# Attention and mixture of experts in one kernel: two buffers for the turned rows of the projections, and the first routing spread over the second attention

## The chip, the cores and the metric

The kernel runs on one NeuronCore of a Trainium2 chip. Its engines are TensorE (PE in the rows; PEld is its weight load), VectorE (DVE), ScalarE (ACT), GpSimd (POOL) and SyncE (SP), which here only issues transfers. Each engine works through its own list of instructions in order, and waits for semaphores that the others raise. The metric is the time of one execution on the device in microseconds, smaller is better. The time before is 1181.86 us, the median of three runs (1181.4 to 1183.72).

## The reference

Two sequences of 2048 rows of 256 values pass through one attention head (width 128, rotary positions), and then twice through a mixture of eight experts with the two best chosen per row:

```python
# x: [2, 2048, 256]
x = x + layernorm(attn(layernorm(x), wq, wk, wv, wo))
x = x + layernorm(ffn(layernorm(x), norm_w, router_w, w1, w3, w2))

# attn: q, k, v = x @ wq.T, x @ wk.T, x @ wv.T; rotary on q, k from the second row on
w = softmax(q @ k.T / sqrt(128)); out = (w @ v) @ wo.T

# ffn, LOOPS = 2 times over z, E = 8 experts, F = 512
z_norm = z * rsqrt(mean(z * z) + 1e-6) * norm_w
scores = softmax(z_norm @ router_w); vals, idx = top_k(scores, 2)
vals = vals / (sum(vals) + 1e-9)
z = z + sum_e vals_e * ((silu(z_norm @ w1[e]) * (z_norm @ w3[e])) @ w2[e])
```

## The kernel before

**Stages.** The first block of the program handles sequence 0 and then sequence 1: projections, then attention. A second block runs the four expert passes (two loops by two sequences, 39 tiles of 128 rows each), which take two thirds of the time and which the change leaves as they are but for names. A sequence is 16 tiles of 128 rows; the projections take them in 8 pairs. Every number that goes through a product is split into two halves of 16 bits, a high one and the rest (`_hi` and `_lo` functions), and each product is made as three matmuls.

**A pair of the projections.** ScalarE normalises two tiles into `xn` (`x_norm`, L760), TensorE transposes them into the bank `psum_t[0]` (`turn_x`, L1225), ScalarE writes the high half of the one buffer `xT` (`x_hi`, L766), VectorE the rest (`x_lo`, L1029). Then come 12 matmuls (`qkv`, L1235) into two banks, one for each tile. From each bank ScalarE takes v (`v_hi`, L772), VectorE the rest of v (L1037) and the products for the rotation (L1045), and GpSimd adds those up (`rotate`, L660, L661). TensorE transposes the turned q and k (`turn_qk`, L1245), ScalarE and VectorE store them as halves (`qk_hi`, L778; `qk_lo`, L1054). On TensorE pair n is written as `qkv(n)`, then `turn_x(n + 1)`, then `turn_qk(n - 1)`: the next pair is transposed only after the matmuls that read `xT`.

In sequence 1 the same pairs also carry work for the experts. ScalarE scales the high halves of two groups of expert weights for each pair (`split_pair`, `split_hi`, L787); the rest of the even group is made on GpSimd (`split`, L671, L675), that of the odd group on VectorE (`split_lo`, L1021). TensorE transposes x for the router (`first_turn`, L540), ScalarE copies it (`copy_zT`, L580), TensorE makes the logits (`logits`, L565). GpSimd computes two roots (L330, L334).

**A step of the attention.** Step t makes the scores of tile t (L1258), transposes the probabilities of tile t - 1 in four groups (`turn_p`, L1253), projects tile t - 2 (L1283) and multiplies the probabilities of t - 1 with v (L1291). VectorE takes the maxima (L1065, L1082), the low halves of the transposed probabilities (`p_lo`, L1060) and the statistics of the result (L1089, L1094). ScalarE makes the exponentials (L832) and high halves (L783, L815), and normalises the result (L818) once GpSimd's chain (`normalise`, L684 to L694) gives the root. GpSimd adds it to x (L696). Steps 3 to 15 are a hardware loop on each engine.

**The first routing.** In the second attention VectorE runs `first_routing` and the five functions of `place` as one block of about 70 small instructions, between its work for steps 0 and 1. ScalarE stands still until it is done:

```python
                if last:
                    exps(act, 0)
                    act.wait_ge(s_eid, 1)
```

Then VectorE marks, for each of 32 halves of tiles, which lane a token goes to (`mark_lanes`, L494): six in step 2 and two in each later step. TensorE sums the marks at the end (`tokens_of_rows`, L502) and VectorE turns the sums into row numbers (`row_indices`, L512 to L518). Meanwhile ScalarE scales each row tile for the experts (`first_row_of`, L802), GpSimd splits it into the one buffer `first_split` (`first_rows`, L706, L708) and SyncE stores it, one tile in each step from step 1 to 16.

## Time and profile before

| | before |
|---|---|
| time, median of 3 runs | 1181.86 us |
| the profiled execution's own time | 1178.43 us |
| its span on the core | 1176.6 us |
| TensorE busy | 1047.3 us, 89% |
| VectorE busy | 738.3 us, 63% |
| ScalarE busy | 579.2 us, 49% |
| GpSimd busy | 530.8 us, 45% |

The shares are means over stages that have different limits. All starts are counted from the start of the span. The projections of sequence 0 run from 14.7 to 51.2 us, the first attention to 190.9, the projections of sequence 1 to 246.6, the second attention to 398.3; the experts take the rest. A number in the clock column below 1.00 means that for a part of that stretch TensorE ran at the lower of its two clocks.

### The profile page before, as it was taken

What the parts mean: (1) busy time and instruction counts of PE and PEld (TensorE: products, weight loads), DVE (VectorE), ACT (ScalarE), POOL (GpSimd) and SP (SyncE); (2) the same over time, 40 slices, a digit from 0 to 9 for tenths busy, and PEclk for the clock granted to TensorE, in tenths of its full rate; (3) what the DMA queues carried; (4) which work ended last, traced back from release to release, by engine and by line L of the source; (5) the groups of instructions that cost most, each with busy time, mean ns of one, the idle gap of its engine ahead of it and who ended that gap; (6) DMA issues with size and microseconds to landing.
All of it is one profiled execution on the core that took longest, in us unless ns stands there. A gap on an engine that the chain in (4) does not pass through costs nothing.

```text
span 1176.6 us, 25481 instructions
## 1 busy us (share of the span) xinstructions
PE 1047.3 (89%) x7762; PEld 705.7 (60%) x7763; DVE 738.3 (63%) x1671; ACT 579.2 (49%) x1124; POOL 530.8 (45%) x699
## 2 busy tenths in 40 slices
PE   5699897758999499999999999999999999999930
PEld 3476675536777366666666666666766666666620
DVE  6799998859999344476345466444467536544436
ACT  4466565627888334453345464344454333333312
POOL 3312234834777553344444444444354444554315
PEclk9999999969999799999999999999999999999975
DMA  9900000000000133354365354355445446433344
GB/s 319 324 1 0 0 0 1 1 0 15 18 15 16 50 74 77 81 143 110 90 162 140 79 141 114 90 136 142 110 125 128 91 121 162 123 92 90 81 141 163
DMA packets 146309, 110.78 MB, mean 94 GB/s; under 512 B 92592, under 2 KB 132144, under 8 KB 146224
## 3 DMA queue, kind: packets, MB, share of 16 engines
q1 hardware_dynamic: 131248, 68.72, 23.2%
q0 software_dynamic: 14976, 40.91, 11.8%
q8 instruction: 55, 0.90, 0.3%
q14 instruction: 30, 0.25, 0.1%
HBM read 56.11 MB, written 33.03 MB: 76 GB/s over the span
## 4 chain that ended last, share of the span: by engine, by line
PE 61%; DVE 2%; DMA 1%; issue 1%; ACT 0%; POOL 0%; ACTq 0%; SPq 0%; DVEq 0%; POOLq 0%
PE psum_s L1869 35%; PE psum_o L1888 17%; PE psum_s L1877 6%; PE psum_t L565 2%; PE psum_t L1831 1%; DVE arena L1661 1%; DMA arena<-expert_rows 0%; DVE f_stats L1687 0%; DMA arena<-arena 0%; DMA arena<-sorted_rows,token_of_row 0%; DVE arena L1667 0%; DMA expert_rows<-arena,result_row_of_row 0%; PE psum_t L502 0%; DVE f_tmp L341 0%; ACT arena L1646 0%
## 5 line engine op out<-in xcount | busy, mean ns | idle before, releaser
L1869 PE MATMUL psum_s<-w_all,arena 128*128 x1872 | 432.8, 381 | 12.1 <-DMA arena<-arena 11.2
L1536 POOL DMA_INDIRECT expert_rows<-arena,result_row_of_row x156 | 157.0, 1007 | 356.7 <-ACT arena L1621 354.9
L1869 PEld LDWEIGHTS psum_s<-w_all,arena 128*128 128x128 f16 x1872 | 174.2, 98 | 212.9 <-issue 22.4
L1791 DVE SCALAR_TENSOR_TENSOR arena<-psum_s,gate_scale,arena 128x512 f32<-128x512 f32 x156 | 117.1, 750 | 205.3 <-PE psum_s L1869 201.2
L1888 PE MATMUL psum_o<-w_all,arena 128*128 x1872 | 229.8, 273 | 1.5 <-DVE arena L1784 1.5
L1888 PEld LDWEIGHTS psum_o<-w_all,arena 128*128 128x128 f16 x1872 | 181.7, 98 | 47.9 <-issue 3.6
L1784 DVE TENSOR_TENSOR arena<-psum_s,arena 128x512 f16<-128x512 f32 x156 | 107.5, 689 | 148.2 <-ACT arena L1610 147.4
L1621 ACT ACTIVATE arena<-psum_o 128x256 f32<-128x256 f32 x156 | 59.8, 383 | 251.3 <-PE psum_o L1888 251.3
L1527 POOL DMA_INDIRECT arena<-sorted_rows,token_of_row x156 | 153.4, 983 | 52.1 <-issue 45.7
L1615 ACT ACTIVATE arena<-psum_s,silu_scale 128x512 f32<-128x512 f32 x156 | 107.2, 687 | 123.1 <-PE psum_s L1869 123.0
L1610 ACT ACTIVATE arena<-psum_s 128x512 f16<-128x512 f32 x156 | 93.1, 597 | 20.0 <-PE psum_s L1877 14.0
L1291 PE MATMUL psum_o<-arena 128*128 128x128 f16 x1536 | 96.6, 220 | 4.1 <-DVE arena L1060 2.0
L832 ACT ACTIVATE arena<-psum_s,arena,alpha 128x1024 f32<-128x1024 f32 x64 | 76.5, 1199 | 38.9 <-DVE arena L1082 38.7
L1291 PEld LDWEIGHTS psum_o<-arena 128*128 128x128 f16 x1536 | 89.4, 98 | 9.6 <-DVE arena L1060 8.8
L1877 PE MATMUL psum_s<-ident,arena 128*128 128x128 f32 x624 | 94.1, 273 | 0.8 <-DVE arena L1791 0.8
L1258 PE MATMUL psum_s<-arena 128*128 128x512 f16 x384 | 91.7, 390 | 1.4 <-DVE arena L1054 1.4
L783 ACT ACTIVATE arena<-psum_t 128x512 f16<-128x512 f32 x128 | 69.9, 595 | 46.3 <-PE psum_t L1253 32.0
L1060 DVE SCALAR_TENSOR_TENSOR arena<-psum_t,arena 128x512 f16<-128x512 f32 x128 | 81.9, 680 | 5.2 <-ACT arena L783 4.8
L1065 DVE TENSOR_REDUCE arena<-psum_s 128x1 f32<-128x1024 f32 x64 | 77.5, 1214 | 8.6 <-PE psum_s L1258 8.6
L1253 PE MATMUL psum_t<-ident,arena 128*128 128x128 f32 x512 | 69.7, 279 | 9.7 <-DVE arena L1060 6.8
L1877 PEld LDWEIGHTS psum_s<-ident,arena 128*128 128x128 f32 x624 | 73.5, 143 | 3.2 <-DVE arena L1791 1.6
L1253 PEld LDWEIGHTS psum_t<-ident,arena 128*128 128x128 f32 x512 | 57.5, 143 | 19.5 <-DVE arena L1060 6.8
(235 smaller groups left out, 1119.6 us busy)
## 6 DMA issues: line engine op xcount, KB each, us to landing
w_all<-in_L_ffn_w SPq DMA_DIRECT2D x24, 512.0 KB, 10.1
arena<-expert_rows SPq DMA_DIRECT2D x48, 256.0 KB, 3.4
sorted_rows<-w_all SPq DMA_DIRECT2D x24, 256.0 KB, 2.6
arena<-expert_rows SPq DMA_DIRECT2D x8, 512.0 KB, 6.0
out<-x_sb SPq DMA_DIRECT2D x8, 512.0 KB, 6.8
...
```

Source lines behind the costliest of these rows:

```text
L1253: last = nc.tensor.transpose(psum_t[g % 2][:, k * P : (k + 1) * P], probs[:, kc * P : (kc + 1) * P], ident[:, :])
L1258: last = nc.tensor.matmul(psum_s[:, kb * 512 : (kb + 1) * 512], qkT[:, lq, 0, bass.ds(i * P, P)], qkT[:, lk, 1, kb * 512 : (kb + 1) * 512] ...
L1291: last = nc.tensor.matmul(psum_o[:, 0:P], v_tiles[:, kc, lv, :], pT[:, lp, at], start=(kc == 0 and k == 0), stop=(kc == NT - 1 and k == 2))
L1527: nc.gpsimd.indirect_dma_start(x_pair[:, u, :, :].rearrange("p l d -> p (l d)"), None, x_split[h], bass.IndirectOffsetOnAxis(ap=sources[:, ...
L1536: nc.gpsimd.indirect_dma_start(expert_rows[h][:, :], bass.IndirectOffsetOnAxis(ap=targets[:, h, t : t + 1], axis=0), y_row[:, u, :], None) ...
L1610: nc.scalar.activation(hT[:, 0, :, :].rearrange("p c t -> p (c t)"), psum_h, ACT.Copy).then_inc(s_h_hi, 1)
L1615: nc.scalar.activation(silu_a, psum_a, ACT.Silu, scale=silu_scale[:, 0:1]).then_inc(s_silu, 1)
L1784: nc.vector.tensor_tensor(hT[:, 1, :, :].rearrange("p c t -> p (c t)"), psum_h, hT[:, 0, :, :].rearrange("p c t -> p (c t)"), ALU.subtract ...
L1791: nc.vector.scalar_tensor_tensor(h_row, psum_b, gate_scale[:, 0:1], silu_a, ALU.mult, ALU.mult).then_inc(s_h, 1)
L1869: last = nc.tensor.matmul(bank, e_xT[:, u, lx * DC + c, :], w_split[:, bass.ds(e * EW + at, FF)], start=(q == 0), stop=(q == 3 * DC - 1))
L1877: last = nc.tensor.transpose(psum_h[:, c * P : (c + 1) * P], h_row[:, c * P : (c + 1) * P], ident[:, :])
L1888: last = nc.tensor.matmul(psum_e, hT[:, lh, c, :], w_split[:, bass.ds(e * EW + at, D)], start=(q == 0), stop=(q == 3 * FC - 1))
```

## The change

- **Two buffers for turned rows.** `xT` becomes a pair of buffers, the second lying where `pT` is in the attention. TensorE is given `turn_x(n + 1)` ahead of `qkv(n)`; ScalarE does `x_hi(n + 1)` ahead of `v_hi(n)` and `x_norm(n + 2)` behind it; VectorE does `x_lo(n + 1)` first.
- **High halves of odd groups.** In the projections of sequence 1 VectorE makes them itself (`split_hi`, seven of them); ScalarE keeps the even ones. They get a semaphore of their own.
- **Scratch for the first routing.** Its tiles no longer share words with probabilities, so they can live through steps. The block is cut up: `first_factors` goes to the end of the projections, the constants and `shifted_logits` behind step 0, the softmax and the first pick behind step 1, the second pick and the gates behind step 2, `tiles_before`, `expert_starts` and `expert_rows_of_tiles` behind step 3, `rows_of_tokens`, `experts_of_tiles` and `mark_tiles` behind step 4. Lanes are marked four in a step, in steps 5 to 12. The sums of tokens and the row numbers come in step 14. Steps 3, 4, 13, 14 and 15 are written out on VectorE and no longer in the loop. ScalarE no longer waits for `s_eid`.
- **Rows for the experts.** `first_split` becomes two buffers; the rows start in step 0, two each in steps 1 and 2, and end in step 13.

```diff
         xn = take(2 * D).rearrange("p (u d) -> p u d", u=2)
-        first_row, first_split = xn[:, 0, :], xn[:, 1, :].bitcast(F16)
-        xT = take(2 * 2 * D // 2).bitcast(F16).rearrange("p (l u c t) -> p l u c t", l=2, u=2, c=DC)
+        first_row = xn[:, 0, :]
+        xT_words = (take(2 * 2 * D // 2), pT[:, 0, :].bitcast(F32)[:, 0 : 2 * D])
+        xT = [w.bitcast(F16).rearrange("p (l u c t) -> p l u c t", l=2, u=2, c=DC) for w in xT_words]
+        first_split = (xn[:, 1, :].bitcast(F16), xT_words[0][:, 0:D].bitcast(F16))
...
+        FIRST_ROWS = [(0,), (1, 2), (3, 4)] + [(i + 2,) if i < NT - 2 else () for i in range(3, NT + 4)]
...
-            v_hi(0, 0)
-            x_hi(1)
-            act.wait_ge(s_shift_x, 2)
-            for i in range(1, PAIRS):
-                if i < PAIRS - 1:
-                    x_norm(i + 1, i + 1)
-                v_hi(i, i)
+            for i in range(PAIRS):
                 if i < PAIRS - 1:
                     x_hi(i + 1)
-                qk_hi(i - 1, i - 1)
+                v_hi(i, i)
+                if i == 0:
+                    act.wait_ge(s_shift_x, 2)
+                if i < PAIRS - 2:
+                    x_norm(i + 2, i + 2)
+                if i:
+                    qk_hi(i - 1, i - 1)
...
+            def split_hi(n):
+
+                if n > 1:
+                    dve.wait_ge(s_w_lo_v, (n - 1) // 2)
+                nc.vector.tensor_scalar(w_split[:, n * 2 * GROUP : n * 2 * GROUP + GROUP], w_raw[:, n * GROUP : (n + 1) * GROUP],
+                                        scale_g[:, :, :].rearrange("p e g -> p (e g)")[:, n : n + 1], None,
+                                        ALU.mult).then_inc(s_w_hi_v, 1)
...
             step(NT, True, False, False, False, False)
-            split_lo(FIRST_SPLITS + 1)
-            first_routing()
-            for place_step in place:
-                place_step(dve, link, 0)
+            routing_constants()
+            shifted_logits(dve, link, 0)
+            split_lo(odd(0))
             step(NT + 1, True, True, False, False, False)
-            split_lo(FIRST_SPLITS + 3)
+            softmax(dve, link, 0)
+            pick_best(dve, link, 0, 0)
+            split_lo(odd(1))
+            step(NT + 2, True, True, True, False, False)
+            pick_best(dve, link, 0, 1)
+            gate_values(dve, link, 0)
+            split_lo(odd(2))
+            step(NT + 3, True, True, True, True, False, 0, read_counts)
+            tiles_before(dve, link, 0)
+            expert_starts(dve, link, 0)
+            expert_rows_of_tiles(dve, link, 0)
+            split_lo(odd(3))
+            step(NT + 4, True, True, True, True, False, 1)
+            rows_of_tokens(dve, link, 0)
+            experts_of_tiles(dve, link, 0)
             dve.wait_ge(s_rows, 1)
             dve.wait_ge(s_marks, 7)
             mark_tiles(first_hot_t)
-            step(NT + 2, True, True, True, False, False)
-            split_lo(FIRST_SPLITS + 5)
-            mark_lanes(first_hot_p, 0, 6)
-            with dve.Fori(3, NT) as i:
+            split_lo(odd(4))
+            with dve.Fori(5, 13) as i:
                 step(NT + i, True, True, True, True, False, i - 3)
-                split_lo(2 * i + FIRST_SPLITS + 1)
-                mark_lanes(first_hot_p, 2 * i, 2)
-            step(2 * NT, False, True, True, True, False, NT - 3)
-            split_lo(2 * NT + FIRST_SPLITS + 1)
-            row_indices(dve, link, 0, token_sums[0])
+                split_lo(odd(i))
+                mark_lanes(first_hot_p, 4 * i - 20, 4)
+            step(NT + 13, True, True, True, True, False, 10)
+            split_lo(odd(13))
+            step(NT + 14, True, True, True, True, False, 11, read_tokens)
+            row_indices(dve, link, 0)
+            split_lo(odd(14))
+            step(NT + 15, True, True, True, True, False, 12)
+            split_lo(odd(15))
+            step(2 * NT, False, True, True, True, False, NT - 3)
+            split_lo(odd(NT))
...
             def pair(n, i):
+                if i < PAIRS - 1:
+                    turn_x(n + 1)
                 qkv(n)
```

How the change moves instructions, first on ScalarE in the projections of sequence 0. These are the rows for pairs 0 to 2 before: L772 is `v_hi`, L766 `x_hi`, L760 `x_norm`, L778 `qk_hi`.

```order
8 L760 ACTIVATE arena<-x_sb,arena 128x256 x2
9 L772 ACTIVATE arena<-psum_s 128x128 x2
10 L766 ACTIVATE arena<-psum_t 128x512
11 L760 ACTIVATE arena<-x_sb,arena 128x256 x2
12 L772 ACTIVATE arena<-psum_s 128x128 x2
13 L766 ACTIVATE arena<-psum_t 128x512
14 L778 ACTIVATE arena<-psum_t 128x2x256
```

The same place after the change, where L809 is `v_hi`, L803 `x_hi`, L797 `x_norm` and L815 `qk_hi`.

```order
8 L797 ACTIVATE arena<-x_sb,arena 128x256 x2
9 L803 ACTIVATE arena<-psum_t 128x512
10 L809 ACTIVATE arena<-psum_s 128x128 x2
11 L797 ACTIVATE arena<-x_sb,arena 128x256 x2
12 L803 ACTIVATE arena<-psum_t 128x512
13 L809 ACTIVATE arena<-psum_s 128x128 x2
14 L797 ACTIVATE arena<-x_sb,arena 128x256 x2
15 L815 ACTIVATE arena<-psum_t 128x2x256
```

`x_hi` has moved ahead of `v_hi`, and `x_norm`, which stood ahead of `v_hi` from pair 1 on, now stands behind it, for a pair one further on.

Second, TensorE in the same stage. Before, L1235 is `qkv`, L1225 `turn_x`, L1245 `turn_qk`:

```order
9 L1235 MATMUL psum_s<-arena 128x384 x12
10 L1225 MATMUL psum_t<-ident,arena 128x128 x4
11 L1235 MATMUL psum_s<-arena 128x384 x12
12 L1225 MATMUL psum_t<-ident,arena 128x128 x4
13 L1245 MATMUL psum_t<-ident,arena 128x128 x4
```

After, L1309 is `qkv`, L1299 `turn_x`, L1319 `turn_qk`; one more `turn_x` stands ahead of row 9:

```order
9 L1309 MATMUL psum_s<-arena 128x384 x12
10 L1299 MATMUL psum_t<-ident,arena 128x128 x4
11 L1309 MATMUL psum_s<-arena 128x384 x12
12 L1319 MATMUL psum_t<-ident,arena 128x128 x4
13 L1299 MATMUL psum_t<-ident,arena 128x128 x4
14 L1309 MATMUL psum_s<-arena 128x384 x12
```

The transposes of the pair that comes next now stand between `turn_qk` and `qkv`, so the second `qkv` waits behind the transposes of the third pair.

Third, VectorE at steps 0 and 1 of the second attention. Before, behind the maxima of step 0 (L1065, L1082) stood the whole routing; these are its first and last rows, and step 1 begins at L1060.

```order
269 L1065 TENSOR_REDUCE arena<-psum_s 128x1 x2
270 L1082 SCALAR_TENSOR_TENSOR arena<-arena,neg_alpha 128x1
271 L1021 SCALAR_TENSOR_TENSOR w_all<-w_all,scale_g 128x512
...
323 L528 TENSOR_SCALAR expert_of<-arena 128x39
324 L1060 SCALAR_TENSOR_TENSOR arena<-psum_t,arena 128x512 x2
```

After, step 0 (L1116, L1133) is followed by the constants and shifted logits, and `p_lo` of step 1 (L1111) comes after ten rows. L1072 is `split_lo`.

```order
279 L1116 TENSOR_REDUCE arena<-psum_s 128x1 x2
280 L1133 SCALAR_TENSOR_TENSOR arena<-arena,neg_alpha 128x1
281 L1156 CAST rank_down<-rank_down 128x8
282 L1157 CAST tile_row<-tile_row 128x39
283 L1158 TENSOR_SCALAR tile_numbers<-tile_row 128x39
284 L416 TENSOR_TENSOR arena<-f_mean,router_sum 128x128
285 L417 TENSOR_TENSOR arena<-psum_y,arena 128x128
286 L418 TENSOR_TENSOR arena<-arena,row_root 128x128
287 L421 TENSOR_REDUCE arena<-arena 128x16
288 L422 TENSOR_TENSOR arena<-arena 128x128
289 L1072 SCALAR_TENSOR_TENSOR w_all<-w_all,scale_g 128x512
290 L1111 SCALAR_TENSOR_TENSOR arena<-psum_t,arena 128x512 x2
```

None of the routing's instructions is gone; the rest of them stand behind `p_lo` of steps 1 to 4.

## Rows read from the trace of the kernel before

**Rows 1.** Windows by stage: length, busy time of each engine (instructions), PEclk, DMA share, GB/s.

```profile
190.90:246.60 55.70, 40.85 (x267) 30.12 (x266) 40.65 (x108) 34.08 (x73) 41.90 (x57) 0.91 0.00 1
246.60:269.50 22.90, 11.77 (x37) 5.68 (x37) 16.85 (x67) 3.41 (x7) 1.12 (x2) 0.62 0.00 0
284.00:384.30 100.30, 99.10 (x1024) 75.75 (x1023) 93.64 (x184) 90.17 (x168) 73.24 (x129) 1.00 0.05 17
```

**Rows 2.** Timeline of TensorE, projections of sequence 0: start, length, line, [idle before].

```profile
20.41 2.12 PE L1235 MATMUL psum_s<-arena 128*128 128x384 f16 x12 [1.41 <-DVE arena L1029]
...
28.94 2.12 PE L1235 MATMUL psum_s<-arena 128*128 128x384 f16 x12 [1.13 <-DVE arena L1029]
...
32.92 2.12 PE L1235 MATMUL psum_s<-arena 128*128 128x384 f16 x12 [0.98 <-DVE arena L1029]
...
44.84 2.12 PE L1235 MATMUL psum_s<-arena 128*128 128x384 f16 x12 [0.98 <-DVE arena L1029]
```

**Rows 3.** Timeline of ScalarE in the same stage.

```profile
21.82 1.09 ACT L760 ACTIVATE arena<-x_sb,arena 128x256 f32<-128x256 f32 x2 [2.19 <-DVE arena L925]
...
31.10 0.28 ACT L772 ACTIVATE arena<-psum_s 128x128 f16<-128x128 f32 x1 [0.70 <-PE psum_s L1235]
...
32.51 1.09 ACT L760 ACTIVATE arena<-x_sb,arena 128x256 f32<-128x256 f32 x2
```

**Rows 4.** Groups of VectorE by shape (busy, mean ns), then timelines of VectorE and GpSimd.

```profile
L1712 DVE TENSOR_SCALAR arena<-x_sb,f_mean,f_rstd x24 | 8.5, 406 | 0.0
```

```profile
211.54 1.02 DVE L341 TENSOR_TENSOR f_tmp<-f_stats 128x16 f32<-128x16 f32 x1
212.48 0.18 DVE L342 TENSOR_TENSOR f_tmp<-f_stats 128x16 f32<-128x16 f32 x1
...
211.03 1.49 POOL L671 TENSOR_TENSOR arena<-w_all,scale_g 128x512 f32<-128x512 f32 x1
```

**Rows 5.** GpSimd: L671 as a whole (ns min/median/max), then its timeline.

```profile
L671 POOL TENSOR_TENSOR arena<-w_all,scale_g x24: 1037/1042/1492, 204.3 to 387.4; 128x512 f32<-128x512 f32 x24
```

```profile
220.25 2.92 POOL L330 TENSOR_TENSOR f_rstd<-f_var,neg_half 128x16 f32<-128x16 f32 x1
...
278.67 1.16 POOL L675 TENSOR_TENSOR w_all<-arena,w_all 128x512 f16<-128x512 f32 x1 [4.67 <-ACT w_all L787]
```

**Rows 6.** Timeline of TensorE around the start of the second attention.

```profile
240.26 1.43 PE L1245 MATMUL psum_t<-ident,arena 128*128 128x128 f32 x4 [2.71 <-POOL arena L661]
...
246.55 4.62 PE L1258 MATMUL psum_s<-arena 128*128 128x512 f16 x12
...
276.90 2.75 PE L1258 MATMUL psum_s<-arena 128*128 128x512 f16 x12
...
284.26 2.75 PE L1258 MATMUL psum_s<-arena 128*128 128x512 f16 x12
```

**Rows 7.** Timeline of VectorE: the last instruction before the routing's block, and the first behind it.

```profile
252.47 0.22 DVE L1082 SCALAR_TENSOR_TENSOR arena<-arena,neg_alpha 128x1 f32<-128x1 f32 x1
...
269.51 1.29 DVE L1060 SCALAR_TENSOR_TENSOR arena<-psum_t,arena 128x512 f16<-128x512 f32 x2 [0.66 <-ACT arena L783]
```

**Rows 8.** Timeline of VectorE: step 2, one step of the loop, start of the last step.

```profile
277.30 1.29 DVE L1060 SCALAR_TENSOR_TENSOR arena<-psum_t,arena 128x512 f16<-128x512 f32 x2
...
283.72 1.42 DVE L494 TENSOR_SCALAR arena<-lane_numbers,lane_of_row,token_numbers 128x128 f16<-128x128 f16 x6
285.06 1.28 DVE L1060 SCALAR_TENSOR_TENSOR arena<-psum_t,arena 128x512 f16<-128x512 f32 x2
...
300.63 1.28 DVE L1060 SCALAR_TENSOR_TENSOR arena<-psum_t,arena 128x512 f16<-128x512 f32 x2
...
308.40 1.29 DVE L1060 SCALAR_TENSOR_TENSOR arena<-psum_t,arena 128x512 f16<-128x512 f32 x2
...
386.00 1.28 DVE L1060 SCALAR_TENSOR_TENSOR arena<-psum_t,arena 128x512 f16<-128x512 f32 x2
```

**Rows 9.** Timeline of ScalarE at the end of the second attention.

```profile
393.23 0.56 ACT L818 ACTIVATE arena<-psum_y,arena 128x256 f32<-128x256 f32 x1 [1.82 <-POOL arena L694]
```

322 lines of the change are left out of this document (181 added, 141 removed).

## The prediction

> **What bounds the kernel now.** I read the windows by stage first, then the timeline of each engine inside the three stages that the change touches. The experts, from 411 us on, are not touched, so whatever is won or lost lies between 14.7 and 398.3 us and is passed on unchanged.
>
> In the projections of sequence 0 the matmuls of one pair start 3.98 us after those of the pair before (28.94 and 32.92), and TensorE stands still for 0.98 us of that, for the low half of the one buffer `xT` [rows 2]. That is the wait which the second buffer is to take away.
>
> In the projections of sequence 1 no engine is full as a mean, but TensorE (40.85 us), VectorE (40.65) and GpSimd (41.90) are each busy for three quarters of 55.7 us [rows 1]. The last transposes, at 240.26, wait for GpSimd for 2.71 us [rows 6].
>
> In the second attention the routing's block keeps VectorE from 252.6 to 269.5 us [rows 7], with TensorE busy for 11.77 of 22.9 us there and its clock at 0.62 as a mean, so mostly at the lower of its two levels, 1.2 GHz [rows 1]. After it, the loop runs with both engines looking full: in 100.3 us TensorE is busy 99.10 and VectorE 93.64 [rows 1]. Which of them sets the pace is the question on which the forecast hangs. One step lasts 7.77 us, from 300.63 to 308.40 [rows 8]. Inside it VectorE never waits for another engine: its idle time is the wait for its own statistics and the issue of addresses. TensorE could go faster: a matmul waiting for its input counts as busy, and the scores of steps 2 and 3 start 7.36 us apart, at 276.90 and 284.26 [rows 6]. So VectorE sets the pace, and what is on VectorE's list there is paid for in full.
>
> **The change part by part.** All sums are against the profiled execution (1178.43 us; span 1176.6); the median of the runs shown, 1181.86, lies 3.4 above it, and I add that at the end.
>
> *Projections of sequence 0.* The second buffer removes the 0.98 us, but the new order on ScalarE puts another chain in its place. `x_norm(n + 2)` now stands behind both `v_hi(n)`, and `qkv(n + 1)` stands on TensorE behind the transposes that need this `x_norm`. From rows: matmuls start at 28.94, the second `v_hi` at 31.10, so 2.16 later; the next instruction on ScalarE goes 0.17 behind it; the two normalisations take 1.09; two transposes are issued in 0.22, and about 0.05 goes on semaphores [rows 2, 3]. Together 3.69 us for a pair where it was 3.98, so 0.29 won and not 0.98. At the beginning it costs: `x_norm` of pair 2 waited until 21.82 for the shifts of the later tiles (released by VectorE) while the matmuls of pair 1 had started at 20.41 [rows 2, 3]. Now these matmuls stand behind that `x_norm`, at about 22.5, 2.1 late. Pair 2 starts 1.4 late, and five periods win back 1.45. The last pair has no transposes ahead of it: its matmuls follow 2.4 us behind those of pair 6, at 43.2 where it was 44.84 [rows 2]. **Sum: 1.6 us won.** Bounds: 0, if the late start is not made good, and 4.9, if TensorE ran without the wait of 0.98 for five pairs.
>
> *Projections of sequence 1.* ScalarE gives seven high halves to VectorE. No such instruction is in the trace. The nearest row is L1712, the same operation over 256 elements, at 406 ns [rows 4]; 256 elements more at one in a cycle of 0.96 GHz (as the two lengths L1712 and the 512-element L1021, 0.75 us, differ) give about 0.67, of which 0.6 counts as a place in the queue. Bounds: 0.4 as for L1712 itself, and 1.4 if it also has to wait for GpSimd. I take 0.6, so 4.2 us in all, on an engine that in the first half of the stage has hardly any room. There I find pair 3 on VectorE where it was. In the second half GpSimd is full: a split takes 1.04 and 1.16 us, seven of them, the rotations 1.65 for a pair, and the two roots 2.92 each [rows 5]. From its first root (220.25) to its last rotation, for which the transposes at 240.26 wait [rows 6], it stands still for only 0.5 us. It can start this stretch about 0.5 earlier, save that wait, and some of the L671 at 1.49 in place of 1.04: **1.3 us won**, with 0 and 4 as bounds (0.98 saved for each of four pairs).
>
> *VectorE through the second attention.* Since it sets the pace, I keep a ledger from the scores (246.55) to the start of the last step (386.00) [rows 6, 8]. The routing's instructions are the same, so moving them is worth nothing in itself. What alters:
> - `first_factors`, three small instructions, leaves: -0.55. The copy of the counts is wider: +0.1. The row numbers come in from behind the last step: +1.3.
> - Five steps are written out. Step 2 before, written out, lasted 7.76 (277.30 to 285.06), of which six marks take 1.35 (1.42 less the overlap) [rows 8]. With 0.4 for statistics of x that makes 6.8. A step of the loop without its two marks (0.45) takes 7.32, so 0.5 each: -2.5. Steps 13 and 15 carry no marks and would end below TensorE's 7.36: +1.1.
> - Two idle stretches around the old block (0.38 for the exponentials, 0.66 in rows 7) go: -1.0. A new wait of 0.5 comes for the first `p_hi`.
> - Step 1 now meets TensorE at the lower clock. The scores took 4.62 us at 246.55 where they take 2.75 at full clock [rows 6]. Before, the block covered this; now VectorE waits for each half: +1.5 (bounds 0 and 2.1).
> - In steps 1 and 2 ScalarE has two row tiles to scale through one `first_row`. The second waits until GpSimd has done its split (1.16 us behind ScalarE's [rows 5]) and the first row, and the high halves of `pT` are queued behind it: +1.2 for both steps. Nothing else hides that, since VectorE's next instruction needs these halves.
> - Contention. The old block ran with GpSimd idle (1.12 us busy of 22.9 [rows 1]). Now some 30 instructions with two inputs in SBUF run beside a GpSimd that is 73% busy [rows 1]. In rows 4 such an instruction of 16 elements took 1.02 us, and ended with GpSimd's L671, while its neighbour took 0.18. I count about four such meetings of 0.7 us, in steps 2 to 4: +2.7. Bounds: 0, and 7, if half of them meet (the block's 5 us of GpSimd work in a step is passed twice).
>
> The lanes marked four at a time cost 0.45 more in each of eight steps and nothing in the others; the count is 32 as before, so that is 0. **Sum: -0.55 + 0.1 + 1.3 - 2.5 + 1.1 - 1.0 + 0.5 + 1.5 + 1.2 + 2.7 = 4.4 us lost.**
>
> The Trainium skill, in SBUF — State Buffer, section SBUF: two separate sides, says that VectorE and GpSimd share a pair of ports as an exclusive lock, held for the whole instruction, and taken on VectorE by instructions with two SBUF inputs or in a mode with two ports. The trace agrees, with L341 at 1.02 us. This speaks against the change: by it the routing and GpSimd's work in the same microseconds add up, the upper bound of 7 above. The skill's VectorE: DVE Perf Modes, section The perf-mode tier table, would give the new high halves two elements in a cycle (fp32 in SBUF), so 0.4 and not 0.67 us; the 406 ns at 256 elements rather looks like one in a cycle. By the page the stage would win 1.9 us more on VectorE, but little on GpSimd, and would take the lock.
>
> *End of the attention.* The last projection waits for L818, and L818 stood still for 1.82 us for GpSimd's chain [rows 9], which was queued behind a row split (1.1 us), while VectorE had the row numbers (1.3 us) in front of its own part. Both are gone from there; of the wait I leave 0.4 for the chain itself: **1.45 us won**. Bounds 0.5 and 1.8.
>
> **Sum.** 4.4 - 1.6 - 1.3 - 1.45 = 0.05 us, so 1178.5 in the profile's terms, and 1181.8 as a median.
>
> **The rivals.** Faster or slower by less than 0.2% (2.4 us) can't be told from no change.
>
> 1. *Forecast: what the projections and the end win, the attention gives back,* 1181.8, own range 1179.5 to 1184.2. Chance 0.38.
> 2. *TensorE keeps its clock and the meetings with GpSimd are rare.* Then 1.5 of step 1 goes, the first scores take 2.75 in place of 4.62 (1.9 won), and contention is 1: 5 us won, 1176.8. It needs TensorE busy through the end of the projections; against it, it waits there for GpSimd as before (2.71 us [rows 6]), and GpSimd's end moves by only 1.3. For it: the attention may have slack that I don't see, since TensorE is 99% busy in the loop too; where TensorE sets the pace, the routing is nearly hidden. Chance 0.35.
> 3. *The port is passed to and fro.* Each of GpSimd's five large instructions in a step holds back one of VectorE's. It decides from about 5 us of lost time over steps 1 to 4, where a block of 3 to 5 us stands in each; at the upper bound of 7 the result is 4.3 worse, 1186. Against it: in the loop GpSimd does small work for 2.6 us behind VectorE's statistics, and only then the large. Chance 0.22.
> 4. *The second buffer does what it says,* so that the pairs of sequence 0 fall to about 3.0 us: 3.3 more won, 1178.5. Only if `x_norm` isn't on the path as I read it. Chance 0.05.
>
> **How the numbers follow.** Faster: rivals 2 and 4 (less a part that stays within 0.2%), 0.37. Same: 0.38. Slower: rival 3 and the upper edge of the forecast, 0.25. The range goes from beneath rival 2, 1175.5, to rival 3, 1186.5; this leaves out its outer parts, about 2 in 10.
>
> **What the profile after would show.** Periods of 3.7 us between the `qkv` of sequence 0, with idle time released by ScalarE's `x_norm` in place of `x_lo`, and the second `qkv` near 22.5. Scores of the second attention near 243.7. No long gap on TensorE at 252 to 262, but VectorE still without gaps, loop steps of 8.2 us (7.77 + 0.45), and its last step near 387.5. In steps 1 to 4 small instructions of VectorE at 0.7 to 1.2 us in place of 0.3. The first fetch for the experts at about 399.4. I am wrong if loop steps with four marks stay near 7.77 (then TensorE set the pace), if pairs of sequence 0 run at 3.0, or if the routing's instructions keep their 0.29 us.

## The result, and the profile after

| | median | lowest to highest | executions |
|---|---|---|---|
| before | 1181.54 us | 1177.9 to 1185.49 | 20 |
| after | 1186.82 us | 1182.75 to 1190.44 | 20 |

The ratio of the two times, after over before, is 1.0043 with a 95% interval of 1.0029 to 1.0057. So the changed kernel is slower by some 5 us (3.4 to 6.7), where no measurable change was forecast, and its median lies just above the range (1186.5). Slower by over 0.2% had a chance of 0.25. The profiled execution took 1184.75 us (span 1183.0), 6.4 us of span above that of before.

The timeline of TensorE in the projections of sequence 0 answers to [rows 2]; L1299 are the transposes of `turn_x` (a turn, for short), L1309 the matmuls of `qkv` (a product). First the first turn of the kernel before, then the kernel after.

```profile
11.48 1.18 PE L1225 MATMUL psum_t<-ident,arena 128*128 128x128 f32 x4 [0.31 <-ACT arena L760]
```

```profile
13.90 1.18 PE L1299 MATMUL psum_t<-ident,arena 128*128 128x128 f32 x4 [0.31 <-ACT arena L797]
17.10 1.09 PE L1299 MATMUL psum_t<-ident,arena 128*128 128x128 f32 x4 [2.02 <-DVE arena L1081]
17.98 3.76 PE L1309 MATMUL psum_s<-arena 128*128 128x384 f16 x12
24.57 1.09 PE L1299 MATMUL psum_t<-ident,arena 128*128 128x128 f32 x4 [2.83 <-ACT arena L797]
25.45 3.44 PE L1309 MATMUL psum_s<-arena 128*128 128x384 f16 x12
...
30.51 2.11 PE L1309 MATMUL psum_s<-arena 128*128 128x384 f16 x12
...
33.57 0.84 PE L1299 MATMUL psum_t<-ident,arena 128*128 128x128 f32 x4 [0.51 <-ACT arena L797]
34.24 2.11 PE L1309 MATMUL psum_s<-arena 128*128 128x384 f16 x12
```

The period is 3.73 us (30.51 to 34.24), and the idle time in it is now released by ScalarE's L797, `x_norm`: as forecast. But look at the second pair. Its matmuls start at 25.45, 11.55 us behind the first transposes, where they stood 8.93 behind in the profile of before, and they take 3.44 instead of 2.12 us. TensorE had stood still for 2.83 us ahead of the transposes at 24.57, and its clock is at the lower level behind that: these transposes take 1.09 where later ones take 0.84. So the third pair comes 5.06 us after the second and not 3.7.

ScalarE's timeline says who is late, as in [rows 3]: the `x_norm` of pair 2, released by VectorE's L967, the shifts of the later tiles.

```profile
23.83 1.09 ACT L797 ACTIVATE arena<-x_sb,arena 128x256 f32<-128x256 f32 x2 [1.77 <-DVE arena L967]
```

Windows over sequence 1's projections, the five written-out steps of attention 2, and the loop with four marks a step: length, busy time and instructions of each engine, PEclk, DMA share, GB/s ([rows 1]).

```profile
193.80:249.10 55.30, 42.01 (x270) 30.58 (x268) 44.56 (x118) 31.02 (x67) 42.28 (x57) 0.88 0.00 1
249.10:303.20 54.10, 44.32 (x350) 30.73 (x350) 46.92 (x108) 32.95 (x61) 24.35 (x42) 0.87 0.06 18
311.40:378.50 67.10, 60.61 (x629) 46.58 (x628) 63.08 (x125) 54.91 (x103) 44.92 (x79) 1.00 0.05 16
```

The new high halves on VectorE (line view of L1064: ns min/median/max), and TensorE at the end of that stage, which answers to [rows 6]: the last transposes still wait for GpSimd.

```profile
L1064 DVE TENSOR_SCALAR w_all<-w_all,scale_g x7: 470/487/1144, 202.9 to 235.7; 128x512 f16<-128x512 f32 x7
```

```profile
242.83 1.42 PE L1319 MATMUL psum_t<-ident,arena 128*128 128x128 f32 x4 [3.15 <-POOL arena L699]
...
249.12 4.86 PE L1332 MATMUL psum_s<-arena 128*128 128x512 f16 x12
```

In the second attention, VectorE (first fence) and GpSimd (second) at the end of step 2:

```profile
276.39 0.25 DVE L454 RECIPROCAL arena<-arena 128x16 f32<-128x16 f32 x1
276.68 0.26 DVE L456 TENSOR_TENSOR arena<-arena 128x16 f32<-128x16 f32 x2
276.98 1.61 DVE L459 TENSOR_SCALAR gates<-arena,y_unscale 128x16 f32<-128x16 f32 x2
278.62 1.71 DVE L1072 SCALAR_TENSOR_TENSOR w_all<-w_all,scale_g 128x512 f16<-128x512 f32 x1
280.25 1.27 DVE L1111 SCALAR_TENSOR_TENSOR arena<-psum_t,arena 128x512 f16<-128x512 f32 x2
```

```profile
276.83 0.72 POOL L734 TENSOR_TENSOR x_sb<-x_sb,arena 128x256 f32<-128x256 f32 x1 [1.23 <-ACT arena L858]
277.52 1.03 POOL L709 TENSOR_TENSOR arena<-w_all,scale_g 128x512 f32<-128x512 f32 x1
278.63 1.15 POOL L713 TENSOR_TENSOR w_all<-arena,w_all 128x512 f16<-128x512 f32 x1
```

Two scalings of 16 elements take 1.61 us, and end (278.59) together with GpSimd's L709 (278.55). Then the low half L1072 takes 1.71 where it takes 0.75 alone, and ends half a microsecond behind GpSimd's L713 (279.78). Until 276.8 GpSimd did small work or none, and VectorE's instructions kept their length.

And one step of the loop with four marks (VectorE, then GpSimd), where [rows 8] had 7.77 us:

```profile
328.43 1.28 DVE L1111 SCALAR_TENSOR_TENSOR arena<-psum_t,arena 128x512 f16<-128x512 f32 x2
...
330.96 1.22 DVE L1116 TENSOR_REDUCE arena<-psum_s 128x1 f32<-128x1024 f32 x1
...
332.21 0.55 DVE L1133 SCALAR_TENSOR_TENSOR arena<-arena,neg_alpha 128x1 f32<-128x1 f32 x1
332.68 1.28 DVE L1111 SCALAR_TENSOR_TENSOR arena<-psum_t,arena 128x512 f16<-128x512 f32 x2
...
336.05 0.98 DVE L520 TENSOR_SCALAR arena<-lane_numbers,lane_of_row,token_numbers 128x128 f16 x4
336.94 0.68 DVE L1111 SCALAR_TENSOR_TENSOR arena<-psum_t,arena 128x512 f16<-128x512 f32 x1
```

```profile
332.07 0.67 POOL L747 TENSOR_TENSOR arena<-arena 128x256 f16<-128x256 f32 x1
```

The step is 8.51 us (328.43 to 336.94), not the 8.2 of the forecast. The negative maximum, L1133, is one element for each partition. It takes 0.55 instead of 0.22 us: GpSimd has begun its subtraction L747 0.14 us ahead of it, and the two end within 0.02 us of each other (332.76 and 332.74). d_copy and j_three_marks below test whether the one causes the other.

At the end, ScalarE's L858 for the last projection, as in [rows 9], and what GpSimd did ahead of it:

```profile
400.79 0.56 ACT L858 ACTIVATE arena<-psum_y,arena 128x256 f32<-128x256 f32 x1 [1.25 <-POOL arena L732]
```

```profile
399.36 1.03 POOL L730 TENSOR_TENSOR arena<-arena,neg_half 128x1 f32<-128x1 f32 x1
```

VectorE's low half of an expert group had begun 0.11 us ahead of that power of one element:

```profile
399.25 0.73 DVE L1072 SCALAR_TENSOR_TENSOR w_all<-w_all,scale_g 128x512 f16<-128x512 f32 x1
```

Stage by stage, after against before: the first transposes 2.4 us later (it scatters by this much between kernels that are alike up to there, from 11.31 to 13.90; what sets it was not looked into); from them to the scores of attention 1 0.7 more; attention 1 the same; sequence 1's projections 0.5 less; attention 2 from its scores to the start of its last step 145.03 where [rows 6, 8] give 139.45, 5.6 more; from there to the last addition to x 10.7 instead of 11.6, 0.9 less; the experts 0.9 less. These make the 6.4 of span.

### The profile page after: what moved, and what is told of

Its sections match the earlier page's. It is cut to its first block, busy times and chain, and to the rows that moved or that the text cites. A ratio compares the mean times of both kernels' runs of the same rounds, so it can differ in the third digit from the quotient of the medians.

```text
span 1183.0 us, 25373 instructions
## 1 busy us (share of the span) xinstructions
PE 1052.2 (89%) x7762; PEld 708.9 (60%) x7763; DVE 748.1 (63%) x1678; ACT 576.3 (49%) x1117; POOL 530.4 (45%) x699
## 4 chain that ended last, share of the span: by engine, by line
PE 61%; DVE 2%; DMA 1%; issue 1%; ACT 0%; POOL 0%; ACTq 0%; SPq 0%; DVEq 0%; POOLq 0%
PE psum_s L1953 35%; PE psum_o L1972 17%; PE psum_s L1961 6%; PE psum_t L600 2%; PE psum_t L1915 1%; DVE arena L1741 1%; DMA arena<-expert_rows 0%; DVE f_stats L1767 0%; DMA arena<-arena 0%; DMA arena<-sorted_rows,token_of_row 0%; DVE arena L1747 0%; PE psum_t L528 0%; DMA expert_rows<-arena,result_row_of_row 0%; DVE f_tmp L357 0%; ACT arena L1726 0%
## 5 line engine op out<-in xcount | busy, mean ns | idle before, releaser
L1111 DVE SCALAR_TENSOR_TENSOR arena<-psum_t,arena 128x512 f16<-128x512 f32 x128 | 82.0, 680 | 5.7 <-ACT arena L820 5.2
L1327 PE MATMUL psum_t<-ident,arena 128*128 128x128 f32 x512 | 70.9, 282 | 16.5 <-DVE arena L1111 10.7
L1116 DVE TENSOR_REDUCE arena<-psum_s 128x1 f32<-128x1024 f32 x64 | 77.5, 1212 | 9.6 <-PE psum_s L1332 9.6
```

Of the source, the lines that this page charges most:

```text
L1327: last = nc.tensor.transpose(psum_t[g % 2][:, k * P : (k + 1) * P], probs[:, kc * P : (kc + 1) * P], ident[:, :])
```

## The experiments

All kernels were timed in groups, each beside the kernel before on one chip, so their ratios to it are compared, not their times. Numbers in brackets behind a ratio are its 95% interval. In the expectations made before the second group of runs, the "147.8 us" of the last step is the start of its second pair of low halves, 2.8 us behind the start of the step. For comparison with them I name the start of the step itself: 145.03 in the first profile of the change.

The stages in the profile of each kernel, in us. A: first transposes of sequence 0 to the scores of attention 1. B: from there to the first transposes of sequence 1. C: from there to the scores of attention 2. D: from there to the start of its last step. E: from there to the last addition to x. In the second column, "changed" is the order of the change in sequence 0, "repaired" the same with f_start's edit; a star stands for the edit that is told with the kernel. One profile of a stage is not exact: n_before is the kernel before a second time, and differs from it by 4.1 us in B, 2.3 in C and 2.4 in D.

```
kernel             seq 0 order  routing        A      B      C      D      E     ratio
before             old          block        39.67  139.56  55.84  139.45  11.57
n_before           old          block        40.24  143.63  58.11  141.89  11.25  1.0001
o_old_all          old          block        39.26  142.67  56.41  138.74  11.59  0.9992
q_old_first        old          block        39.68  139.52  55.28  139.62  11.55  0.9988
b_block            changed      block        40.37  143.63  55.85  139.51  11.59  1.0016
l_start_block      repaired     block        38.08  141.03  55.42  139.96  11.27  0.9984
the change         changed      four marks   40.41  139.51  55.30  145.03  10.68  1.0043
m_again            changed      four marks   41.02  139.33  55.45  145.95  10.70  1.0046
a_old_projections  old          four marks   40.21  139.21  56.63  144.28  10.19  1.0051
c_low_first        changed      four marks   40.11  142.62  55.31  145.90  10.69  1.0071
g_scalar_split     changed      four marks   40.56  139.59  56.24  143.94  10.20  1.0033
f_start            repaired     four marks   38.07  139.25  55.36  145.90  10.68  1.0007
d_copy             changed      four marks*  40.10  142.62  55.32  142.39  10.69  1.0032
h_olo_late         changed      four marks*  41.02  143.61  55.40  148.89  10.68  1.0065
i_start_olo        repaired     four marks*  38.06  139.07  55.56  148.97  10.68  1.0043
j_three_marks      changed      three marks  41.03  143.60  55.35  141.53  10.04  1.0011
k_start_three      repaired     three marks  38.09  140.95  55.38  142.01  10.05  0.9999
p_old_three        old          three marks  39.88  142.37  57.05  140.94  11.61  0.9998
```

**Undo one half, or the other.** a_old_projections puts back the orders of both sequences' projections and the odd high halves on ScalarE. b_block puts the first routing back as a block.

```diff
--- a_old_projections (TensorE, pair)
-                if i < PAIRS - 1:
-                    turn_x(n + 1)
                 qkv(n)
...
+                if i < PAIRS - 1:
+                    turn_x(n + 1)
                 if i:
                     turn_qk(n - 1)
--- b_block (VectorE)
             step(NT, True, False, False, False, False)
+            split_lo(odd(0))
             routing_constants()
             shifted_logits(dve, link, 0)
-            split_lo(odd(0))
-            step(NT + 1, True, True, False, False, False)
             softmax(dve, link, 0)
...
```

> The change with its projections put back: qkv ahead of the next turn on TensorE, the old order on ScalarE and VectorE in both sequences, and the odd expert groups' high halves on ScalarE again; the spread routing stays. Theory 1 (the loss lies in attention 2, the projections are nearly neutral: 0.7 us lost in sequence 0, 0.5 won in sequence 1): 1186.5 us, as the change within 1 us, 5 us above the kernel before; scores of attention 2 near 3 us earlier than 249.1 only if the weight loads come as in the profile of before. Theory 2 (the projections are what lost, since TensorE's clock fell at the second pair's product): 1181.5 to 1183 us. The forecast's own terms (2.9 us won in the projections) would give 1189.5 us.

> The change with its first routing put back as one block between steps 0 and 1 of attention 2, marks at 6 and then 2 a step, first rows one a step from step 1, token sums at the end; the new projections and the new scratch stay. Theory 1: the 5 us of the loss go with the spreading, so 1181.5 us (1180.5 to 1182.5). Theory 2: 1185 to 1187 us, as the change. The forecast's own terms would give 1179 us.

Measured: 1.0051 (1.0034 to 1.0067) and 1.0016 (1.0002 to 1.0031). The loss goes with the spreading: D is 144.3 in a_old_projections, which keeps it, and 139.5 in b_block, which doesn't. The new projections as they stand win nothing: the kernel with them and the block is, if anything, above the kernel before, where the forecast's own terms gave 2.9 us less for them. Both speak for theory 1 over theory 2, though b_block came out somewhat higher than theory 1 had it.

**ScalarE's wait for the low half.** In steps 2 to 4 of the change ScalarE waits up to 3.2 us for VectorE's low half of the group before, which lies behind the routing's piece, and the first rows and two of the high halves of `pT` are queued behind it. c_low_first takes the low half ahead of the routing's piece in steps 0 to 4; here it is for step 2.

```diff
             step(NT + 2, True, True, True, False, False)
+            split_lo(odd(2))
             pick_best(dve, link, 0, 1)
             gate_values(dve, link, 0)
-            split_lo(odd(2))
```

> The change with VectorE's low half of the odd expert group taken ahead of the routing piece in each of steps 0 to 4, not behind it. Theory 1 (ScalarE's next high half waits for it, 3.2, 2.1 and 1.6 us in steps 3 to 5, and the first rows and the last two high halves of the probabilities wait behind that): the waits are gone, steps 3 to 5 take 10.9, 10.8 and 11.0 instead of 11.85, 11.47 and 11.53 us, 1184.8 us in all (1184 to 1185.5). Rival (VectorE is busy all the time in these steps, so the order of its pieces and ScalarE's wait cost nothing): 1186.8 us, steps unchanged.

Measured: 1.0071 (1.0055 to 1.0087), and the rival was right that nothing is to be had there. The three steps (which begin at 268.40, 280.25 and 291.72 in the change) took 34.24 us together instead of 34.85, but what lies ahead of them took more, and D is 145.90, as in m_again (145.95). VectorE has work all that time, so the wait lies beside it; that this is why it cost nothing is my reading, not a test. The meetings with GpSimd that slow VectorE did not go with the low halves but fell on others: L444 is late by 0.93 us, L491 by 0.83, L459 by 0.67. That the ratio is above the change's own is not explained: in its one profile B is 3.1 us longer than in the change, by the clock of attention 1 that the last group of runs is about, but the timed executions need not share that.

**The meeting in the loop.** d_copy replaces GpSimd's subtraction, L747, by a second copy, which is shorter (0.40 us for 0.67). It leaves out a part of the computation: what is stored as the low half of a row is then no remainder.

```diff
-                nc.gpsimd.tensor_tensor(half[:, D : 2 * D], first_row, half[:, 0:D], ALU.subtract).then_inc(s_first_step, 1)
+                nc.gpsimd.tensor_copy(half[:, D : 2 * D], first_row).then_inc(s_first_step, 1)
```

> The change with GpSimd's subtraction of a first row's low half replaced by a second copy of the row (the low halves stored are then copies, not remainders: that part of the computation is changed). Theory 1 (VectorE's one-element negative maximum, 0.55 instead of 0.22 us in the steps with four marks, stands behind that subtraction for the SBUF port): it is back at 0.22, these steps take 8.2 instead of 8.5 us and the kernel 1184.2 us (1183.5 to 1185). Rival (four marks cost 0.37 us each pair in any case, by VectorE's own time): steps stay at 8.5 and the time at 1186.8 us.

VectorE and GpSimd in one step:

```profile
344.19 1.28 DVE L1111 SCALAR_TENSOR_TENSOR arena<-psum_t,arena 128x512 f16<-128x512 f32 x2
...
347.97 0.27 DVE L1133 SCALAR_TENSOR_TENSOR arena<-arena,neg_alpha 128x1 f32<-128x1 f32 x1
...
352.42 0.68 DVE L1111 SCALAR_TENSOR_TENSOR arena<-psum_t,arena 128x512 f16<-128x512 f32 x1
```

```profile
347.37 0.40 POOL L745 CAST arena<-arena 128x256 f16<-128x256 f32 x1
347.83 0.40 POOL L747 CAST arena<-arena 128x256 f16<-128x256 f32 x1
```

The negative maximum again starts 0.14 us behind GpSimd's L747, and again ends with it (348.24 and 348.23), but now this is after 0.27 us; the step takes 8.23. So it is held until GpSimd's instruction ends, by a copy as by a subtraction, and the shorter one holds it less. The kernel before has the same in its loop, 0.24 us beside a copy. D is 142.39, 2.6 us less than in the change's first profile, as theory 1 said. The ratio, 1.0032 (1.0018 to 1.0047), moves by half of that, within its interval.

**A detour that fails.** h_olo_late takes 0.28 us out of VectorE's way to the negative maximum, in the eight steps with four marks.

```diff
                 if new:
                     half_max(t, 0)
-                if fin:
...
+                if fin and not late:
+                    o_lo(t)
                 if new:
                     half_max(t, 1)
...
+                if late:
+                    o_lo(t)
                 if turn:
                     p_lo(t - 1, 2)
```

> The change with VectorE's low half of the attention output placed behind the negative maximum in the eight steps with four marks (0.28 us that then lies behind it). Theory A (the negative maximum stands 0.33 us behind GpSimd's subtraction for the port because the two extra marks brought the two to one moment): the negative maximum is back at 0.22 us, these steps take 8.2 instead of 8.5 us, the last step comes 145.3 us after the scores instead of 147.8, the kernel 2.4 us less. Rival 1 (the meeting passes to the next instruction on the port): steps stay at 8.5. Rival 2 (TensorE then waits 0.3 us for the late half before its projection and passes that on): 8.4 to 8.5 us.

Measured: 1.0065 (1.004 to 1.0089), steps of 8.75 us, D at 148.89. TensorE and GpSimd show both rivals at once:

```profile
338.29 0.50 PE L1364 MATMUL psum_y<-arena 128*128 128x256 f16 x3 [1.23 <-DVE arena L1121]
```

```profile
336.79 1.15 POOL L713 TENSOR_TENSOR w_all<-arena,w_all 128x512 f16<-128x512 f32 x1
337.89 0.40 POOL L745 CAST arena<-arena 128x256 f16<-128x256 f32 x1
```

TensorE waits 1.23 us for the late half, with the other matmuls of the step queued behind it; all engines shift against each other, and the negative maximum (337.49, 0.47 us) now stands behind L713. The 0.3 us that I had allowed for the wait is near its value in the old order (0.40 in the change's loop), not in the new one.

**Three marks a step.** j_three_marks puts two marks in step 5 and three in each of the ten behind it, and takes the sums in the last step.

```diff
-            with dve.Fori(5, 13) as i:
+            step(NT + 5, True, True, True, True, False, 2)
+            split_lo(odd(5))
+            mark_lanes(first_hot_p, 0, 2)
+            with dve.Fori(6, NT) as i:
                 step(NT + i, True, True, True, True, False, i - 3)
                 split_lo(odd(i))
-                mark_lanes(first_hot_p, 4 * i - 20, 4)
...
+                mark_lanes(first_hot_p, 3 * i - 16, 3)
...
```

> The change with two marks in step 5 and three in each of steps 6 to 15 instead of four in steps 5 to 12, and the sums of the marks taken in step 16 instead of step 14. Theory A (with four marks VectorE comes to its negative maximum 0.14 us after GpSimd has begun the subtraction; a mark less and it comes 0.1 us ahead of it): the negative maximum takes 0.22 to 0.3 us, steps 7.75 + 0.25 = 8.0 to 8.05 us, the last step 3 us earlier (144.8 us after the scores), less 0.2 to 0.5 us at the end, 2.3 us less than the change in all. Rival (any mark beyond two brings the meeting): steps 8.25 us, last step at 147.2 to 147.5, no gain beyond 0.5 us.

```profile
339.32 1.28 DVE L1111 SCALAR_TENSOR_TENSOR arena<-psum_t,arena 128x512 f16<-128x512 f32 x2
...
343.10 0.22 DVE L1133 SCALAR_TENSOR_TENSOR arena<-arena,neg_alpha 128x1 f32<-128x1 f32 x1
...
347.28 0.69 DVE L1111 SCALAR_TENSOR_TENSOR arena<-psum_t,arena 128x512 f16<-128x512 f32 x1
```

```profile
343.19 0.67 POOL L747 TENSOR_TENSOR arena<-arena 128x256 f16<-128x256 f32 x1
```

VectorE comes to its negative maximum 0.09 us ahead of GpSimd's subtraction, takes 0.22 us, and the step is 7.96. D is 141.53, 3.5 to 4.4 less than in the two profiles of the change, and the ratio 1.0011 (0.9993 to 1.0029) against 1.0046 in the same group of runs: 4 us. One mark of 0.25 us more in a step costs 0.55.

**The start of sequence 0.** f_start puts back one order: the second product ahead of the third turn.

```diff
-                if i < PAIRS - 1:
+                if i < PAIRS - 1 and n != 1:
                     turn_x(n + 1)
                 qkv(n)
+                if n == 1:
+                    turn_x(2)
```

> The change with one order of TensorE put back: the second product of sequence 0 stands ahead of the third turn again (all other pairs keep the turn first). Theory A (the projections of sequence 0 won nothing because the third turn waits for the shifts of the second part of x, the second product stands behind it, TensorE idles 2.8 us there and its clock falls): the second product starts some 9 us after the first turn instead of 11.5, takes 2.1 instead of 3.1 to 3.6 us, and the scores of attention 1 come 37.5 to 38.5 us after the first turn instead of 40.1 to 40.4; the kernel 2 us less than the change. Rival (the third turn's wait only moves, x_norm of pair 2 sets the pace anyway): the scores stay 40 us after the first turn, the time the change's.

```profile
17.42 3.01 PE L1309 MATMUL psum_s<-arena 128*128 128x384 f16 x12
21.62 2.11 PE L1309 MATMUL psum_s<-arena 128*128 128x384 f16 x12 [1.20 <-DVE arena L1096]
24.00 0.84 PE L1299 MATMUL psum_t<-ident,arena 128*128 128x128 f32 x4 [0.27 <-ACT arena L797]
...
27.20 2.11 PE L1309 MATMUL psum_s<-arena 128*128 128x384 f16 x12
```

The second product starts 8.3 us behind the first transposes (13.34 to 21.62) and at the upper level; A is 38.07, 2.3 less than in the change and 1.6 less than before. The ratio is 1.0007 (0.9989 to 1.0025), some 4 us below the change's, twice what was expected. 2.3 of it are in A; no other stage of the profile shows the rest, to which I come back below. i_start_olo has both edits:

> Both edits of the two kernels above (second product ahead of the third turn in sequence 0; the output's low half behind the negative maximum in the steps with four marks). Theory A: the gains add, 4 to 4.5 us less than the change, so within 1 us of the kernel before. Rival: they don't add or one of them is nothing, 2 to 2.5 us less than the change, or as the change.

Its ratio is 1.0043 (1.0025 to 1.006); the start is won again (A is 38.06) and the detour loses again (D is 148.97), so the parts add, with a loss where I expected a gain.

**Who should make the odd high halves.** g_scalar_split leaves the orders and puts the high halves of the projections back on ScalarE.

```diff
                     split_even(i - 1)
+                    if i == 1:
+                        split_hi(1, s_w_hi_v)
+                    else:
+                        split_odd(i - 1)
...
-            split_hi(1)
             pair(n0 + 1, 1)
             split_lo(1)
...
```

> The change with the odd expert groups' high halves in the projections of sequence 1 on ScalarE again, behind the even ones; all orders of the change stay. Theory A (VectorE's half costs it 0.5 to 0.6 us a pair and ScalarE had room; what sequence 1 waits for in its second half is GpSimd): first turn to scores 55.3 us as in the change, within 0.4, the time within 1 us. Rival (ScalarE's load is what the move relieved, so 0.7 us a pair come back): 57 to 59 us from first turn to scores, and 2 to 4 us more in all.

C is 56.24 instead of 55.30, and the ratio 1.0033 (1.0015 to 1.0052). The move is worth 0.9 us of C, between theory and rival; the time can't tell it from nothing. What C wins is given back later: with four marks a step and the halves on ScalarE, D is 143.94 and 144.28 and E 10.20 and 10.19 (here and in a_old_projections), with them on VectorE D is 145.03 to 145.95 and E 10.68 to 10.70. The rows show the meetings with GpSimd falling on other instructions: here neither L492 nor the low half behind it is late in step 3.

**The change again, both repairs, and one part alone.**

> The change itself once more, beside the three kernels below on one chip, and with a second profile. Expected by all theories: ratio 1.003 to 1.006, the last step of attention 2 147.8 us after its scores. What is open: the first step of attention 1 at 6.84 us with TensorE at the upper level, as in the first profile of the change, or at 8.3 us with the scores ahead of it at the lower level, as in three of the five kernels that had its projections.

> The change with both repairs: the second product ahead of the third turn in sequence 0, and three marks in steps 6 to 15. If they add: 3 to 3.6 us (the first) and 2.3 us (the second) less than the change, 1180.5 to 1181.5 us where the kernel before takes 1181.3. If the first repair's gain was mostly chance of the clock at the start of attention 1: 1182.5 us.

> The new projections with the second product ahead of the third turn, and the first routing as one block as before: what the projections' part of the change is worth by itself once repaired. Theory A (the block kernel lay 1.9 us above the kernel before for its projections, and the repair is worth 2.3 us by attention 1's scores and up to 3.6 us in the time): 1.5 us less than the kernel before, 1179.8 us where it takes 1181.3 (ratio 0.9975 to 1.0). Rival (the two-buffer projections give nothing in any order): ratio 1.000 to 1.002.

m_again is the change, word for word: 1.0046 (1.0025 to 1.0067), the same result a second time. k_start_three: 0.9999 (0.9987 to 1.0011), 5.5 us below the change: the two repairs together take back the whole loss, and no more. l_start_block is f_start's edit on b_block: 0.9984 (0.9971 to 0.9998), the best kernel here, 1.9 us below before. So the spreading, even repaired, wins nothing that can be told over the block, and what the change has to give lies in its projections.

**Is the lower level at the start of attention 1 the change's doing?** Theories P and Q are put in the expectations below. In five of the eight profiles with the changed order B was 142.6 or more, and TensorE's first scores of attention 1 took 4.45 us or more instead of 2.76. None of the six others then at hand had such a B, though the two last of them, k_start_three and l_start_block, had scores of 4.45 us and a B of 141. Four more kernels with the old order of sequence 0 were run for it: the kernel before; o_old_all, with everything put back but the scratch; p_old_three, a_old_projections' projections with j_three_marks' attention; q_old_first, b_block with sequence 0 alone put back:

```diff
-                if i < PAIRS - 1:
+                if i < PAIRS - 1 and n >= PAIRS:
                     turn_x(n + 1)
                 qkv(n)
+                if i < PAIRS - 1 and n < PAIRS:
+                    turn_x(n + 1)
```

> The kernel before once more, for a second profile of sequence 0. Ratio 1.000 by all theories. Theory P (the change's order of the first two products makes the lower level at the start of attention 1 likelier): 39.4 to 40.3 us from the first turn to the scores and 139.0 to 139.7 us from there to the first turn of sequence 1. Theory Q (the level there is chance in any order): 142.5 to 143.7 us for the second stretch in about half of the profiles of the old order too, this one among them or not.

> Everything put back in the order of before (projections of both sequences, odd high halves on ScalarE, the first routing as a block); what is left of the change is its scratch, the two turn buffers' places and the factors taken earlier. Both theories: ratio 0.999 to 1.001, attention 2 at 139.5 us from scores to the last step. Theory P: 139.0 to 139.7 us from scores to the first turn of sequence 1. Theory Q: 142.5 to 143.7 in half of such profiles.

> The old projections with the spread routing at three marks a step. If the spreading with the meeting removed gives 1.2 us of loss in attention 2's steps 1 to 4 and the end gives 1.5 us back, this is the kernel before within 0.1%: ratio 0.999 to 1.002. If three marks cost as four: 1.004. Theories P and Q as above: 139.0 to 139.7, or 142.5 to 143.7 in half of such profiles.

> The block routing, the old orders in sequence 0 and the new ones with VectorE's odd high halves in sequence 1: the second sequence's part of the change alone. First turn to scores 55.3 us instead of 55.8 to 56.6: ratio 0.999 to 1.0 (0.5 to 1.3 us won). Rival (block routing behind new projections loses it again): ratio 1.0015, as the kernel with the block and all new projections. Theories P and Q as above.

Three of the four have a B of 142.3 or more too (p_old_three with the fall only behind the scores). TensorE at the scores of attention 1 in n_before, then windows there (PEclk behind the busy times), and the window of the change:

```profile
51.76 5.30 PE L1258 MATMUL psum_s<-arena 128*128 128x512 f16 x12 [1.42 <-DVE arena L1054]
```

```profile
51.00:56.00 5.00, 4.24 (x10) 1.50 (x11) 1.92 (x2) 0.00 (x0) 0.00 (x0) 0.50 0.93 297
```

```profile
54.00:59.00 5.00, 2.76 (x12) 1.09 (x12) 3.30 (x5) 0.37 (x1) 0.00 (x0) 1.00 0.61 194
```

So the strict form of theory P falls: the lower level is met in the old order too (three of six profiles, five of eight with the changed order, none of the four with the repaired one, where B is 141.03 at most). It is worth 3 to 4 us in the span, and it scatters the times of both kernels. Whether an order makes it likelier, these few profiles can't tell. The mean granted clock of every timed execution is on record, and it leans to theory P. In the 10 executions of q_old_first it lies between 0.959 and 0.963, in the 12 of b_block, which differs in sequence 0 alone, between 0.953 and 0.961, and at 0.956 or less in 8 of them. The slow second product is in this mean, but as an estimate the 4 us at the lower level there (24.57 to 28.89 in the change) take only 0.002 off it. A clock of 0.958 or less is found in 10 of 20 executions of the change and in one of 12 of f_start; the kernel before has it in 29 of its 115 executions in the four groups of experiments. Against this stands a_old_projections, with the old order, none of six such clocks, and a ratio as high as the change's. It stays open.

The ratios of these four are 1.0001 (0.9989 to 1.0013), 0.9992 (0.9977 to 1.0007), 0.9998 (0.9985 to 1.001) and 0.9988 (0.9973 to 1.0003). None of the four differs from before by more than its interval, so the scratch costs nothing that can be told, nor do three marks with the old projections, and sequence 1's part alone may win a little (C is 55.28 where the old orders have 55.84 to 58.11).

## Why the prediction was wrong

*The projections of sequence 0: the step that failed most.* The sum had 1.6 us won (by its own terms 1.5: the last product comes at 22.5 + 5 x 3.69 + 2.4 = 43.35, not at 43.2). The periods came as forecast (3.73 for 3.69), and so did the late second product (11.55 us behind the first transposes; 11.0 in the forecast). What failed is "Pair 2 starts 1.4 late, and five periods win back 1.45". TensorE stood still for 2.83 us ahead of the third turn, and the third turn and the second product behind it ran at the lower level, which the sum had put at nothing; the third product came 5.06 us behind and not 3.7. Over all profiles A is 39.8 as a mean with the old order (six), 40.6 with the changed (eight): 0.8 lost, 2.4 away from the sum. f_start, which takes that one wait away, gives 38.1: the 1.6 to 1.75 us that the sum had put down to the order as it was.

*Sequence 1.* 1.3 us forecast; 0.5 between the two profiles, and 1.4 between the means of C (five with the old orders 56.8, twelve with the new 55.4). Without the C of n_before, the longest of all, it is 1.1. The term holds within this scatter. GpSimd bounds the second half, as said: the last transposes wait 3.15 us for it. The high half on VectorE was mis-sized: 0.67 us by the row, 0.47 to 0.49 measured (and the two lengths that the prediction compares, 0.406 and 0.75, differ by 0.34, not 0.27; they are different operations). The Trainium skill's VectorE: DVE Perf Modes, section The perf-mode tier table, had it at two elements in a cycle, and the trace agrees with that better than with one.

*Attention 2.* 4.4 us lost were forecast, 5.6 came in the profiled pair (5.2 between the means of D: 145.0 in the five profiles of rows marked "four marks" without c_low_first, and 139.9 in six with the block). The contention in it was forecast at 2.7, in steps 2 to 4 alone. It measured more, and in two places. In steps 2 to 4 five instructions are late by 3.8 us together: L459 by 1.24 (1.61 against the 0.37 of b_block), the three L1072 by 0.97, 0.67 and 0.47 (against 0.74), L492 by 0.45 (0.74 against 0.29). The other routing instructions keep their 0.29 us, which I had named as a sign of being wrong; the meetings are few and long. Against this stands 0.7 that the block had at its own negative maximum in step 1. In the loop, where the forecast had "so that is 0" for marks four at a time, the negative maximum is late by 0.33 us in each of eight steps: 2.7. So contention is 5.8 by the rows, and the other terms of the ledger, +1.7 in the forecast, came to about nothing. Which of them was too high is not settled. d_copy and j_three_marks show the loop's part; that of steps 2 to 4 rests on the rows beside GpSimd's, since no kernel took it away alone; L459 is late by 1.23 or 1.24 us in eleven of the twelve profiles with the spread routing, all but c_low_first's.

The lock of the Trainium skill's SBUF — State Buffer, section SBUF: two separate sides, is borne out: in every loop step with four marks of the change VectorE's negative maximum ends within 0.02 us of GpSimd's subtraction, and in d_copy within 0.02 us of the copy in its place. It bites harder than I had allowed: the negative maximum, one element, is held until a GpSimd instruction of 0.67 us is done.

*The end.* 1.45 won were forecast, 0.9 came (1.0 between the means of E). L858 still waits 1.25 us for GpSimd, because the one-element power ahead of it, L730, takes 1.03 instead of 0.55 beside VectorE's L1072 (399.25 to 399.98). In a_old_projections the same low half begins only 0.04 us ahead of the power, which then keeps its 0.55, and E is 10.19 instead of 10.68:

```profile
396.85 0.76 DVE L1076 SCALAR_TENSOR_TENSOR w_all<-w_all,scale_g 128x512 f16<-128x512 f32 x1
```

```profile
396.89 0.55 POOL L730 TENSOR_TENSOR arena<-arena,neg_half 128x1 f32<-128x1 f32 x1
```

So GpSimd is held by VectorE as well, and 0.07 us in the order of arrival decide about 0.5 us.

*The rivals.* Rival 3, the port, had the right cause for most of the loss, with a chance of 0.22. That its time, 1186, came out is in part luck: it wanted 5 to 7 us lost in steps 1 to 4, where 3.8 were lost, while 2.7 more came in the loop and 0.8 at the start of sequence 0, where its sum, too, had 1.6 won. It set "against it" what was for it: that GpSimd does its large work after the small. VectorE's long piece of routing reaches into just that. Rival 2 is refuted: VectorE sets the pace, and the steps grow with its marks. Rival 4 as well.

*Sum.* Forecast -1.6 - 1.3 + 4.4 - 1.45 = 0.05. Measured by the means of the stages (A, C, D, E) +0.8 - 1.4 + 5.2 - 1.0 = 3.6, by the time 5.1. Of the 3.55 us between the two sums 2.4 are the start of sequence 0, 0.8 attention 2 and 0.45 the end, less 0.1 for sequence 1. The 1.5 us that the time has beyond the stages lie within its interval (3.4 to 6.7). B is 0.65 higher as a mean in the profiles with the changed order; if that order does make the lower level in attention 1 likelier, more of the 1.5 lies there, which is not shown.
